# First attention gate of a four-layer graph network: pair order, three-slot ring, eight product buffers

## What is computed

```
def _gate(h, q, Wg, bg, Wq, bq):            # B=8 groups, N=8 nodes, L=64 queries, F=768
    hg = einsum('bnf,gf->bng', h3, Wg[:, :F])
    qg = einsum('blf,gf->blg', q, Wg[:, F:]) + bg
    attn = sigmoid(hg[:, :, None, :] + qg[:, None, :, :])      # 64 nodes x 64 queries x 768
    qi = einsum('bnlf,blf->bnf', attn, q)
    alpha = sigmoid(h3 @ Wq[:, :F].T + qi @ Wq[:, F:].T + bq)
    return alpha * tanh(qi) + (1 - alpha) * h3

h = relu(rgcn(x, W_rel1, W_root1, b1)); h = _gate(h, ...)      # first gate
h = relu(rgcn(h, W_rel2, W_root2, b2)); h = _gate(h, ...)      # second gate
x = layernorm(x + h)                                           # then three more graph layers
```

## Time and profile before

| | us |
|---|---|
| median of 3 runs (lowest, highest) | 270.37 (269.51, 270.51) |
| the profiled execution | 270.35 |
| its span, first to last instruction | 268.5 |
| first gate, first add to end of the last reduction | 68.08 to 115.89 |
| second gate, the same | 146.65 to 184.46 |

### The profile page before, as it was taken

The page is one execution under the profiler, slowest core; times in us unless marked ns, Lnnn a source line. Parts: engine busy times, 40 slices in busy tenths (PEclk is TensorE's granted clock), DMA queues, the critical chain, the costliest instruction groups (busy, mean ns, idle before and its releaser), DMA issues.

```text
span 268.5 us, 4957 instructions
## 1 busy us (share of the span) xinstructions
PE 251.3 (94%) x2065; PEld 130.9 (49%) x2065; DVE 158.6 (59%) x283; ACT 91.5 (34%) x155; POOL 86.3 (32%) x76
## 2 busy tenths in 40 slices
PE   8899999999999999899999998889998988999994
PEld 4565874454435543356775222224573443435572
DVE  0866450015999999943015999996567267514422
ACT  2323340033657996412001667672302013013000
POOL 7790000003599999700000677870000000000000
PEclk9999999999999999999999999999999999999999
DMA  7999996996002967500699940003999636000001
GB/s 242 373 402 400 402 362 211 379 400 269 2 0 61 410 236 256 102 2 0 163 407 401 402 158 2 0 2 94 363 405 401 264 99 256 0 2 0 2 0 29
DMA packets 21895, 53.46 MB, mean 199 GB/s; under 512 B 4201, under 2 KB 4969, under 8 KB 21874
## 3 DMA queue, kind: packets, MB, share of 16 engines
q1 hardware_dynamic: 21184, 52.82, 53.6%
q10 hardware_dynamic: 690, 0.34, 0.5%
HBM read 52.17 MB, written 0.20 MB: 195 GB/s over the span
## 4 chain that ended last, share of the span: by engine, by line
PE 57%; POOL 17%; DVE 13%; issue 6%; ACT 4%; DMA 2%; SPq 0%; POOLq 0%; DVEq 0%; ACTq 0%
POOL prod L609 13%; PE ps L1137 12%; PE ps L1105 10%; PE ps L1253 6%; POOL W L609 4%; PE ps L1152 4%; PE ps L1079 3%; PE ps L1525 3%; PE ps L1605 3%; PE ps L1222 3%; DMA qn<-in_L_gnn_query_embs 2%; ACT pre L689 2%; DVE prod L905 2%; DVE pre L913 2%; PE ps L1343 2%
## 5 line engine op out<-in xcount | busy, mean ns | idle before, releaser
L609 POOL TENSOR_TENSOR prod<-pre,qn 128x768 f32<-128x768 f32 x28 | 56.0, 2023 | 11.5 <-ACT pre L689 11.5
L913 DVE TENSOR_TENSOR pre<-ps,qg 128x768 f32<-128x768 f32 x46 | 42.9, 950 | 2.0 <-PE ps L1329 0.9
L689 ACT ACTIVATE pre<-pre 128x768 f32<-128x768 f32 x46 | 38.7, 847 | 11.9 <-DVE pre L913 11.1
L1253 PE MATMUL ps<-W 128*128 128x384 f32 x96 | 34.7, 490 | 0.8 <-DVE W L457 0.5
L457 ACT COPY W<-ps 128x384 f32<-128x384 f32 x41 | 18.4, 483 | 39.4 <-PE ps L1079 39.2
L689 ACT ACTIVATE ps<-ps 128x768 f32<-128x768 f32 x18 | 14.2, 794 | 29.6 <-PE ps L1329 21.4
L1343 PE MATMUL ps<-prod,rsel 128*32 128x384 f32 x192 | 20.5, 496 | 3.4 <-POOL prod L609 2.7
L1253 PEld LDWEIGHTS ps<-W 128*128 128x128 f32 x96 | 17.3, 190 | 10.7 <-issue 2.0
L1137 PE MATMUL ps<-W,prod 128*64 128x256 f32 (+1 forms) x240 | 20.6, 328 | 0.0
L1079 PE MATMUL ps<-ident,W 128*128 128x128 f32 x144 | 19.7, 278 | 0.6 <-DMA W<-in_L_gnn_Wg 0.6
L1079 PEld LDWEIGHTS ps<-ident,W 128*128 128x128 f32 x144 | 16.9, 143 | 4.1 <-issue 1.3
(11 more groups left out here) (242 smaller groups left out, 333.8 us busy)
## 6 DMA issues: line engine op xcount, KB each, us to landing
W<-in_L_gnn_W SPq DMA_DIRECT2D x9, 2304.0 KB, 11.8
W<-in_L_gnn_W_rel SPq DMA_DIRECT2D x6, 2304.0 KB, 15.8
W<-in_L_gnn_W_root SPq DMA_DIRECT2D x2, 2304.0 KB, 9.5
W<-in_L_gnn_Wq SPq DMA_DIRECT2D x4, 1152.0 KB, 7.9
W<-in_L_gnn_Wg SPq DMA_DIRECT2D x3, 1152.0 KB, 13.2
qn<-in_L_gnn_query_embs SPq DMA_DIRECT2D x4, 384.0 KB, 10.2
W<-in_L_gnn_Wg SPq DMA_DIRECT2D x3, 384.0 KB, 3.9
W<-qg SPq DMA_DIRECT2D x2, 384.0 KB, 4.9
```

Of the source, the lines that this page charges most:

```text
L609: nc.gpsimd.tensor_tensor(prod_of(T), pre_of(T), qn[:, pair_and_node(t)[0], :], ALU.mult).then_inc(prod_p, 1)
L689: nc.scalar.activation(tile, tile, ACT.Sigmoid).then_inc(sig_ready, 1)
L913: nc.vector.tensor_tensor(dst, ring(T), by_half(qg[:, pair_and_node(T % TILES)[0], :]), ALU.add).then_inc(pre_ready, 1)
L1253: ins = nc.tensor.matmul(ps[:, unit_bank(u), 0:HD], qT[:, k, p * P:(p + 1) * P], WgT_q[:, k, c * HD:(c + 1) * HD], start=(k == 0), stop=(k ...
```

## The change

The first gate takes the form of the second. In detail:

- left(layer, k) and right(layer, k), the ring of three slots, `add_nodes_rows` and eight product buffers now serve both gates. `stack` and the copies into it are gone; DVE makes `low` in one subtraction.
- KINDS of the first gate: 19 tiles P, 13 tiles X. All DVE multiplies read PSUM.
- PE's other work is placed by cycle k. UNIT_IN: query chunks (3,3,3,3,2,2,2), now of units 5, 6 and 7, all inside the gate. LATE_IN: Wq groups, one in cycle 7, two in each of 8 to 11, one in 12. Five more (HIDDEN) are turned before the gate, three (TAIL) at its end. ALPHA_IN: alpha chunks, two in each of 13 to 15.
- Wq groups inside the gate all use bank 7 (TRB), so each waits for the copy of the one before it. The first waits for unit 7's copy, which uses the same bank. Of a cycle's groups, the first stands ahead of `add_nodes_rows`, the second behind.
- rel2_0, rel2_1, rel2_2 go to slots 2, 5, 3. rel2_2 is loaded after the last reduction of the first gate, since slot 3 holds products until then. The copy of qg (qs) is loaded after rel2_2 is used up.
- POOL's bias work waits for DVE's one-hot matrices (hot_ready).

The core of the diff:

```diff
-            ("Wq_h", 5, 2), ("Wq_q", 6, 2), ("rel2_0", 3, 1), ("rel2_1", 2, 1), ("rel2_2", 5, 1), ("root2", 6, 1),
+            ("Wq_h", 5, 2), ("Wq_q", 6, 2), ("rel2_0", 2, 1), ("rel2_1", 5, 1), ("rel2_2", 3, 1), ("root2", 6, 1),
...
-        POOL_TILES = [t * 3 // 2 for t in range(20)]
-        KINDS = ["P" if t in POOL_TILES else "V" for t in range(TILES)] + list(
-            "DP" "DP" "XP" "DP" "XP" "DP" "XP" "DP" "XP" "DP" "XP" "DP" "XP" "DP" "XX" "DD")
+        KINDS = list("XP" "XP" "PP" "XP" "XP" "PP" "XP" "XP" "PP" "XP" "XP" "PP" "XP" "XP" "XP" "XX"
+                     "DP" "DP" "XP" "DP" "XP" "DP" "XP" "DP" "XP" "DP" "XP" "DP" "XP" "DP" "XX" "DD")
...
+        HIDDEN = (5, 2, 3, 6, 7)
+        TAIL = (4, 0, 2)
+        LATE0 = len(EARLY) + len(HIDDEN)
+        TAIL0 = 2 * GROUPS - len(TAIL)
+        LATE_IN = (0, 0, 0, 0, 0, 0, 0, 1, 2, 2, 2, 2, 1, 0, 0, 0)
+        ALPHA_IN = (0, 0, 0, 0, 0, 0, 0, 0, 0, 0, 0, 0, 0, 2, 2, 2)
...
+        UNIT_IN = (3, 3, 3, 3, 2, 2, 2, 0, 0, 0, 0, 0, 0, 0, 0, 0)
...
             link(nc.gpsimd.memset(biases[:, :], 0.0))
+            pool.wait_ge(hot_ready, 3)
...
@@ ScalarE, the loop over a gate's tiles
+                for i in range(TILES):
+                    T = SIGMOIDS[layer * TILES + i]
+                    k = (i - 1) // 2
+                    if layer == 0 and k > 0:
+                        for n in late_of(k)[:1] if i % 2 else late_of(k)[1:]:
+                            copy_group(act, G_QH + n, turned_out_s)
...
                     nc.scalar.activation(tile, tile, ACT.Sigmoid).then_inc(sig_ready, 1)
+                    if layer == 0 and k > 0 and i % 2 == 0:
+                        for u in units_ended(k):
+                            unit_copy(u)
...
@@ VectorE, a gate's adds and multiplies (waits for the query units left out)
+                multiply(left(layer, 0))
+                for k in range(1, HALF_T):
+                    if k == HALF_T - 1 and KINDS[right(layer, k)] == "X":
+                        add(right(layer, k))
+                    multiply(left(layer, k))
+                    multiply(right(layer, k - 1))
+                    if k + 1 < HALF_T:
+                        if KINDS[left(layer, k + 1)] != "D":
+                            add(left(layer, k + 1))
+                        add(right(layer, k))
+                multiply(right(layer, HALF_T - 1))
...
@@ TensorE
-                elif g0 + k >= G_QH + len(EARLY):
-                    wait_group_out(pe, g0 + k - 2)
+                elif G_QH + LATE0 < g0 + k < G_QH + TAIL0:
+                    wait_group_out(pe, g0 + k - 1)
...
+                for k in range(1, HALF_T):
...
+                    if k >= LAG:
+                        reduce_pair(left(0, k - LAG), k == LAG, False)
+                    if k > 0 and late_of(k) and late_of(k)[0] == LATE0:
+                        wait_units_out(pe, UNITS)
+                    turn_wq(late_of(k)[:1])
+                    wait_slot_free(pe, left(0, k - 1))
+                    if k + 1 < HALF_T:
+                        wait_slot_free(pe, right(0, k - 1))
+                        add_nodes_rows((left(0, k + 1), right(0, k)))
+                    else:
+                        add_nodes_rows((right(0, k),))
+                    for u, c in unit_chunks(k):
+                        query_unit(u, [c])
+                    turn_wq(late_of(k)[1:])
...
+                wait_added(pe, right(0, HALF_T - 2))
+                add_bias_alpha(0, 1)
+                for n, k in enumerate(range(HALF_T - LAG, HALF_T)):
+                    project_alpha(0, 1, nodeT, WqT_h, range(2 * n, 2 * n + 2))
+                    if k == HALF_T - 1:
+                        turn_wq(range(TAIL0, TAIL0 + 1))
+                    reduce_pair(left(0, k), False, k == HALF_T - 1)
+                turn_wq(range(TAIL0 + 1, TAIL0 + 2))
```

More of the change, by code:

```diff
@@ L299, in wait_sigmoid @@
             eng.wait_ge(sig_ready, SIGMOIDS.index(T) + 1)
-        def count(kinds, T):
-            return sum(k in kinds for k in KINDS[:T])
         def on_pool(T):
-            return KINDS[T] in POOL_MUL
-        def pool_tiles(T):
-            return count(POOL_MUL, T)
-        IN_PRE = [T for T in range(2 * TILES) if KINDS[T] in IN_SBUF]
+            return KINDS[T] == "P"
         def pre_of(T):
-            return pre[:, IN_PRE.index(T) % PRES, :]
+            return pre[:, POOLED.index(T) % PRES, :]
         def pair_and_node(t):
@@ L376, in gnn_kernel @@
         EARLY = (0, 1, 2, 5, 6, 7)
-        LATE = 2 * GROUPS - len(EARLY)
-        LATE_AT = sorted([13 + 2 * k for k in range(LATE - GROUPS)] + [TILES - KC - GROUPS - 1 + k for k in range(GROUPS)])
+        HIDDEN = (5, 2, 3, 6, 7)
[4 more added lines that the diff above has]
+        ALPHA_IN = (0, 0, 0, 0, 0, 0, 0, 0, 0, 0, 0, 0, 0, 2, 2, 2)
+        assert LATE0 + sum(LATE_IN) == TAIL0 and sum(ALPHA_IN) == KC
         V_UNITS = [(k, c) for k in range(KC) for c in range(2)]
@@ L387, in alpha_psum, with late_of, alpha_of @@
             return ps[:, alpha_bank(layer, part), 0:CUT if part == 0 else HD - CUT]
-        ALPHA_AT = {TILES - KC + k: k for k in range(KC)}
-        def late_groups(t):
-            return len(EARLY) + sum(at < t for at in LATE_AT)
+        def late_of(k):
+            at = LATE0 + sum(LATE_IN[:k])
+            return range(at, at + LATE_IN[k])
+        def alpha_of(k):
+            at = sum(ALPHA_IN[:k])
+            return range(at, at + ALPHA_IN[k])
         def group_bank(g):
@@ L503, in _ @@
             load("Wq_q", Wq[:, D:2 * D], rgcn_done, 2)
-            load("rel2_0", a["L0_gnn_W_rel2"][0], rgcn_done, R + 1)
-            load("rel2_1", a["L0_gnn_W_rel2"][1], qg_done, UNITS)
-            load("rel2_2", a["L0_gnn_W_rel2"][2], turned, G_QH + GROUPS)
-            load("root2", a["L0_gnn_W_root2"], turned, G_END)
+            load("rel2_0", a["L0_gnn_W_rel2"][0], qg_done, UNITS)
+            load("rel2_1", a["L0_gnn_W_rel2"][1], turned, G_QH + GROUPS)
             sp.wait_ge(qk_cleared, 1)
@@ L513, in _ @@
                              allow_slow_non_contiguous=True).then_inc(qk_loaded, 16)
+            load("rel2_2", a["L0_gnn_W_rel2"][2], reduced, TILES // 2)
+            load("root2", a["L0_gnn_W_root2"], turned, G_END)
             done = R + 1
-            sp.wait_ge(rgcn_done, done + 1)
+            sp.wait_ge(rgcn_done, done + R)
             for c in range(2):
@@ L588, in _ @@
             for layer in range(2):
-                for i, (part, ready, stacked) in enumerate(((hi, hi_ready, hi_stacked), (mid, mid_ready, mid_stacked))):
-                    if layer == 1:
-                        break
-                    pool.wait_ge(ready, 1)
-                    for h in range(2):
-                        nc.gpsimd.tensor_copy(stack[i * GN:(i + 1) * GN, h, 1, :],
-                                              part[h * N + GN:h * N + 2 * GN, :]).then_inc(stacked[1], 1)
-                        pool.wait_ge(stacked[1], h + 1)
                 if layer == 1:
@@ L601, in _ @@
                     nc.gpsimd.tensor_tensor(low[:, 0:CUT], t1[:, 0:CUT], mid[:, 0:CUT], ALU.subtract).then_inc(low_ready, 1)
-                for t in range(TILES):
-                    T = layer * TILES + t
-                    if not on_pool(T):
+                for T in POOLED:
+                    if T // TILES != layer:
                         continue
@@ L1352, in second_gate @@
                 pe.wait_ge(mid_ready, 2)
-                pe.wait_ge(low_ready, 2)
-                add_nodes_rows((left(0), right(0)))
-                add_nodes_rows((left(1),))
+                pe.wait_ge(low_ready, 3)
+                add_nodes_rows((left(1, 0), right(1, 0)))
+                add_nodes_rows((left(1, 1),))
                 add_bias_alpha(1, 0)
```

212 lines of the change are left out of this document (86 added, 126 removed).

## The result

| | before | after |
|---|---|---|
| median of 4 runs | 269.96 us (269.51 to 270.51) | 274.74 us (274.49 to 274.94) |
| span of the profiled execution | 268.5 us | 272.7 us |

The ratio is 1.0169, 95% interval [1.0156, 1.0182]: the change makes the kernel 1.7% slower. The forecast was 274.1 us, its range 269.3 to 276.5. TensorE's granted clock is full in both profiles (0.999 and 1.000 of 2.4 GHz), so the clock has no part in the difference.

The account below looks back on a forecast made before the run. DVE was taken to set the first gate's pace. Against 270.35 us, -0.5 - 1.5 - 3.2 + 1.6 + 1.7 + 3.3 + 0.5 + 1.6 + 0.25 = +3.8 gave 274.1 us, range 269.3 to 276.5.

Parts of the forecast that it names:

- front: Before the gate: POOL's bias work held back behind DVE's two products, removing PE's 0.53 us wait for DVE; -0.5 us.
- way in: Start of the first gate: one DVE subtraction instead of four, first add at 66.6 instead of 68.08 us; -1.5 us.
- pace undisturbed: First gate, nothing disturbing DVE: cycles of 2.70 us, 2.60 with a left P tile; 43.6 instead of 46.8, -3.2 us.
- cycles 3 to 6: First gate: PE's rows, chunks and reduction take 3.36 us against DVE's 2.70 in cycles 3 and 4; with 5 and 6, +1.6.
- cycle 7: First gate: Wq group ahead of the rows waits for ACT's copy of unit 7; next add at 4.4, not 2.70; +1.7 us.
- cycles 9 to 12: First gate: groups ahead of the rows wait for ACT's copies behind left sigmoids; left adds 3.5 us apart, not 2.70; +3.3.
- end: End of first gate: right(15) added 0.5 us late, last reduction 1.7 us after the last multiply, not 0.15; +0.5 and +1.6.
- behind the gate: After the first gate: a group and its copy replace two idle-filling products, second alpha chunk needs the second block; +0.25 us.
- under 3 us: Sign for the first gate: the forecast is wrong if DVE's idle time before its adds stays under 3 us.
- Rival 2: First gate: only the copies' chain is wrong, ACT's copies come in time, the 3.3 goes; 270.8 us; chance 0.14.
- Rival 1: First gate: DVE unhindered, PE and ACT get everything done under DVE; 265.4 us; chance 0.17.

Follow-up runs that it names:

- d1: The kernel before with only POOL's bias work made to wait for DVE's three one-hot tables; 269.72 us, ratio 0.9986.
- a2: The changed kernel with the single Wq group of cycle 7, and its wait for unit 7's copy, behind that cycle's row products; 273.15 us, ratio 1.0119.
- c1: The changed kernel with Wq groups two a cycle in 8 to 12, around the reduction, and ACT's group and unit copies reordered around the sigmoids; 270.12 us.
- c7: c6 with query chunks 4, 3, 2, 2, 1, 2, 2, 2 over cycles 0 to 7 and Wq groups in cycles 9 to 13; 268.28 us, ratio 0.9931.
- c3: c1 with query chunks 4,3,3,2,2,2,2, alpha's first part in cycles 13 and 14, two second-part chunks and a group behind the last reduction; 269.1 us.
- c4: c1 with query chunks 4,3,3,2,2,2,2, right(15)'s rows before that cycle's reduction, alpha in cycles 14 and 15, its second part before the last three reductions; 269.92 us.
- c6: c4 with the first part's alpha chunks two to a cycle in 13 to 15 again; 269.12 us, ratio 0.9962.

## Why the prediction was right, step by step

| term | predicted | trace of after |
|---|---|---|
| front | -0.5 | -0.83 (`hi` cast at 62.77, before 63.60); d1 alone -0.62 |
| way in, cast of `hi` to first add | -1.5 | 3.09 against 4.48: -1.39 |
| pace undisturbed | -3.2 | 2.66 to 2.71 a cycle wherever nothing else holds: -3.0 |
| cycles 3 to 6 | +1.6 | distances 3.52, 3.51, 2.87, 2.87: +2.0 |
| cycle 7 | +1.7 | 4.53: +1.8 |
| cycles 9 to 12 | +3.3 | 3.43, 3.43, 3.50, 3.42: +3.0 |
| end | +2.1 | left(15) to last reduction 6.98, undisturbed 4.65: +2.3 |
| behind the gate | +0.25 | last reduction to the alpha projection of qi: +0.12; no wait of PE for a weight of rel2 |
| sum | +3.8 | last reduction +4.03, start of the alpha projection of qi +4.15, spans +4.2 |

The sum was set on the execution of 270.35 us; the ratio of the result makes the change +4.6, the two spans, by which the table goes, +4.2. From the first add to the last reduction it took 53.21 us, before 46.96: +6.25 against a predicted +5.5. The four stall terms cost 9.2 us where I had 8.7, and the undisturbed pace gave 3.0, not 3.2: cycles with a P tile on the left ran at 2.66 where I had 2.60. The terms miss by 0.1 to 0.4 us each and in both directions, so part of the sum's closeness is their cancelling. The range of 7 us holds even an unchanged time; what bears out the mechanism is the single distances, and the edits below.

**Right, and shown by an edit.** Cycle 7 (a2: 1.5 us by itself; the other 0.3 of its 1.8 are PE-bound, as in cycles 3 to 6), cycles 9 to 12 (c1: with cycle 7, 4.5 us of the gate), the front (d1), and the whole: c7 has the changed tiles and none of the large stalls, and is faster than before.

**One sign was missed.** DVE was to idle 6 to 8 us before its adds, and it idled 11. The 6 to 8 are the stalls alone (1.6 + 1.7 + 3.3 + 0.5 = 7.1). The wait of 0.85 behind each of the four P tiles on the left, which belongs to the undisturbed pace, and 0.94 before the first add come on top: c7, with no large stall, still idles 4.8 us there. So idle time of the pacing engine isn't loss by itself, and "under 3 us" could not have served as a sign of being wrong.

**The front was under-sized.** I took PE's 0.53 of idle for the term and 0.6 as the most that could come; 0.62 came in the trace of d1 and 0.83 in the execution of after, where a wait for a load of Wg was also shorter (0.34 against 0.55 us). The traces of the changed kernel and its edits, all with the same front, put the cast of `hi` anywhere from 62.73 to 63.21, so differences of up to 0.5 here are those of executions; where they come from, but for that load, isn't shown.

**The PE-bound cycles were under-sized.** In cycles 3 and 4 the distance was 3.5, not 3.36: rows to chunk 0.60, three chunks 2.13, reduction 0.79. Between row products and what follows the rows show 0.60 where three steps of 0.165 make 0.49: 0.1 for a change from 32-row to 128-row products, the same before a query chunk, a group and a reduction. The prediction had this one. It had nothing for two more: the last product of the chunks lasts 0.42 us up to the reduction and not 0.32, and the first one behind the rows 0.43. This is the price that the prediction set beside the rule of the Trainium skill (TensorEngine Tiling (Array Packing), Key Properties), that a change of mode drains the engine: the trace agrees in that every such change costs, and the cost is small. The rule spoke less against this change than the prediction has it. The kernel before had no 32-row products, but it paid the same 0.1 between its products of 128*128 or 96*128 and its reductions of 128*32.

**The end was right, by its own sum.** Behind the rows of right(15) I had 5.2 us of PE's work up to the last reduction; it took 5.3 (113.75 to 119.07), without a gap. The runs c3, c4 and c6 show what such an end is: moving right(15) forward (c4) or work behind the reduction (c3) changed who waited and hardly the time, and only what goes into PE's idle time in earlier cycles is won. My expectations for these runs, not the prediction, took it for a matter of waits.

**Rival 2** (only the copies' chain wrong, 270.8 us) put its finger on the place where the change could be mended; with cycle 7 mended too it is c1, 270.1. **Rival 1** (DVE unhindered, 265.4) stays out of reach even for c7: two of its assumptions, no PE-bound cycles and an end on DVE's heels, are still broken there, by 0.8 us (left distances of 2.87 to 3.03 in four cycles) and 1.9 us (6.6 from left(15) to the last reduction, not 4.65), and PE in that kernel is busy 45.68 of the 48 us from 66 to 114.

## What to carry to other kernels

A faster instruction on the engine that sets the pace is worth what the other engines' written order lets through: here 3 us of pace and 1.4 us of a shorter way in were paid for with 9 us of waits for each other's answers and behind queues. For each cycle write down, from the pacing engine's instruction, the chain copy, product, answer that the next one needs; work with a bank of its own that must be copied out (groups, units) goes where the copying engine is idle, around a long operation of PE, and no cycle may hold the end of one user of a bank and the start of the next. Near a stage's end add up what PE has still to do behind its last input, before looking at who waits.
